# Paths as a nine-row product on TensorE, a reordered opening, later outputs and a third side buffer in a convolution stage

## Chip, cores and metric

One core of one Trainium2 chip runs the whole program. Its engines are TensorE (PE, with its weight loads as PEld), VectorE (DVE), ScalarE (ACT), GpSimd (POOL) and SyncE (SP, which issues all DMAs); each works through its own instructions in program order and waits on semaphores for the others. The metric is the device time of one execution in microseconds (us).

## What is computed

64 sequences of 128 tokens and 256 features pass through a cross attention, a mixture of experts, an alignment with a context and a convolutional feed-forward block, each added to the residual `x`. The change lies in the last two:

```python
def _align_one(small, large):
    D = _pairwise_euclidean(small, large)
    R = _dtw_cost(D)                       # dynamic time warping
    i_idx, j_idx, valid = _backtrack(R, T_small, T_large)
    contrib = small[i_idx] * valid[:, None].astype(small.dtype)
    return jnp.zeros((T_large, d), dtype=small.dtype).at[j_idx].add(contrib)
...
def _L1_ffn_ref(x, w1, conv_w, conv_b, w2):
    h = bit_linear(x, w1)                  # rows quantised to 8 bits, ternary weights
    h = depthwise_conv1d(h.transpose(0, 2, 1), conv_w, conv_b)   # 3 taps
    h = jax.nn.silu(h.transpose(0, 2, 1))
    return bit_linear(h, w2)
...
x = x + _L1_xattn_ref(ctx_1024, _layernorm(x, axis=-1))
x = x + _L1_ffn_ref(_layernorm(x, axis=-1), L1_ffn_w1, L1_ffn_conv_w, L1_ffn_conv_b, L1_ffn_w2)
```

The path of a sequence crosses column t between two bounds. So the alignment's result is a product of the context with a 128 x 128 matrix of zeros and ones (`path_sb`): an entry is 1 where the column number lies between that token's lower and upper bound. Tokens' bounds are neighbouring entries of one table, `entries` (64 sequences x 129).

## The kernel before

Four stages follow one another: attention, experts, `align` (the warping table row by row on DVE, then the way back), and `conv_ffn`. The change touches the last two.

**The end of `align`.** The table is compared in eight chunks of 16 rows. For a chunk, DVE writes `falls` and then `left` (`compare`), PE sums both with `places` into two banks (`gather`, L1536 and L1542), DVE scans the 1024 columns of both banks (`trace`, L1657), PE takes differences (`differ`), ACT copies them (`rises`), and after the last chunk DVE walks back through 128 rows (L1692). Chunks 0 to 6 lie beside the table's rows; the last one stands alone.

**The convolution.** The 64 sequences are 16 groups of four (`GB = 4`, `NG = 16`), and the 1024 hidden features are 8 tiles, so a step n is tile m = n % 8 of group g = n // 8. All engines run the same loop `for n in STEPS`, and at step n each does its own part of a software pipeline: PE makes hidden tile n (`hidden`, L1869) and turns tile n-4 (`turn_hidden`, L1879); ACT makes the middle and side taps of tile n-1 (`taps`, L2003 and L2007) and the SiLU of n-3 (L2014); DVE adds the left tap of n-2 (`tap`, L2145), takes the maxima of tile n-5 (L2150) and scales tile n-14 (L2171); POOL adds the side of n-2 (`add_side`, L2251) and rounds tile n-15 (L2259). The remaining work of a group is hung on certain values of m:

- the path of group g+3, all on ACT: `path_distance` (m = 0, L1952, four ops of 128 columns), `path_gap` (m = 2, L1960, four more), `path_entry` (m = 4, L1969, one op of 512);
- `expand(g, half)` on PE multiplies path and context (L1843), at m = 7 and m = 1; DVE adds it to `x_all` (`add_expanded`) and takes the moments, POOL the inverse deviation, ACT normalises (`normalise`, L1978, m = 5), DVE finds the scale (`find_scale`, m = 6), ACT scales up (`scale_up`, m = 7), POOL scales back (`whole_units`), PE transposes (`turn`, m = 2 and 5), ACT and DVE split it into a leading and a trailing part (L1995, L2137);
- the outputs: `output` on PE (L1904, 16 matmuls, m = 7 of group g+2 and m = 1 of g+3), `weigh_out` on ACT, `finish` on POOL (L2274), `store` on SP. `hidden_scale` on DVE (m = 4) writes the hidden scale and its inverse `inv2`, in two buffers.

Ahead of the loop stands an opening, in which groups 0, 1 and part of 2 are prepared. PE's order there is `expand(0,0)`, `expand(0,1)`, `expand(1,0)`, `turn(0,0)`, `turn(0,1)`, `expand(1,1)`, `expand(2,0)`, and only then the first `hidden`. ACT makes the paths of groups 0 and 1, the leading parts of group 0, then `normalise(1)`, `scale_up(1)` and the path of group 2. A `side` buffer (two of them) is free again when POOL has added it; the bank `ex_ps` is shared by all `expand` calls but one.

## Time and profile before

| what | value |
|---|---|
| median of 3 runs | 3388.7 us (3388.69 to 3393.39) |
| the profiled execution's own time | 3391.26 us |
| its span, first to last instruction | 3389.5 us |
| busy share of the span | PE 91%, DVE 72%, ACT 53%, POOL 38% |
| mean granted TensorE clock | 0.956 of full speed |
| last instruction of `align` to the end | 2957 us to 3389.5 us |

The shares are averages over four stages. In attention and experts PE is busy throughout; in the convolution it isn't. All positions in time below are microseconds from the span's start.

### The profile page before, as it was taken

What the parts mean: (1) busy time and instruction counts of PE and PEld (TensorE: products, weight loads), DVE (VectorE), ACT (ScalarE), POOL (GpSimd) and SP (SyncE); (2) the same over time, 40 slices, a digit from 0 to 9 for tenths busy, and PEclk for the clock granted to TensorE, in tenths of its full rate; (3) what the DMA queues carried; (4) which work ended last, traced back from release to release, by engine and by line L of the source; (5) the groups of instructions that cost most, each with busy time, mean ns of one, the idle gap of its engine ahead of it and who ended that gap; (6) DMA issues with size and microseconds to landing.
All of it is one profiled execution on the core that took longest, in us unless ns stands there. A gap on an engine that the chain in (4) does not pass through costs nothing. (4 is left out here: it accounts for less than half of the span.)

```text
span 3389.5 us, 63898 instructions
## 1 busy us (share of the span) xinstructions
PE 3082.9 (91%) x23092; PEld 2669.3 (79%) x23092; DVE 2443.4 (72%) x5410; ACT 1787.2 (53%) x4638; POOL 1296.7 (38%) x1194
## 2 busy tenths in 40 slices
PE   6999999999999999999998999999999953158887
PEld 5888888888888888888887888888888841046665
DVE  5666666666666666666666787878787759769998
ACT  5565655555555555555554333333333326179996
POOL 2333333333333333333332333333333320058886
PEclk9999999999999999999999999999999975589999
DMA  5000000000000000000001112121212151011101
GB/s 159 5 8 5 8 5 8 5 7 5 8 5 8 5 8 5 8 5 8 4 5 57 58 51 64 51 66 50 65 54 61 58 80 42 1 31 38 50 32 38
DMA packets 108535, 103.81 MB, mean 31 GB/s; under 512 B 26560, under 2 KB 87488, under 8 KB 108224
## 3 DMA queue, kind: packets, MB, share of 16 engines
q1 hardware_dynamic: 108224, 99.72, 10.2%
q8 instruction: 188, 3.08, 0.4%
q14 instruction: 123, 1.01, 0.1%
HBM read 86.55 MB, written 13.14 MB: 29 GB/s over the span
## 5 line engine op out<-in xcount | busy, mean ns | idle before, releaser
L794 POOL TENSOR_TENSOR attention_prob<-attention_prob,attention_inv_sums 128x1024 f32<-128x1024 f32 x256 | 479.6, 1894 | 399.8 <-DVE attention_inv_sums L652 399.8
L504 ACT ACTIVATE attention_prob<-attention_turns,attention_neg_max 128x256 f32<-128x256 f32 x1024 | 467.6, 482 | 175.3 <-DVE attention_neg_max L643 175.3
L1371 POOL TENSOR_TENSOR experts_hidden_lo<-experts_weighed,experts_hidden_hi 128x512 fp32r<-128x512 f32 x192 | 255.0, 1328 | 531.4 <-ACT experts_hidden_hi L1124 531.4
L659 DVE COPY attention_probT<-attention_turns 128x512 f32<-128x512 f32 x512 | 329.0, 684 | 163.1 <-PE attention_turns L380 163.0
L346 PE MATMUL attention_turns<-kv_hi,wkv 128*128 128x512 f32 x1024 | 374.1, 406 | 0.0
L643 DVE TENSOR_REDUCE attention_neg_max<-attention_turns 128x2 f32<-128x512 f32 x512 | 318.1, 684 | 45.2 <-PE attention_turns L370 44.3
L1124 ACT ACTIVATE experts_hidden_hi<-experts_weighed 128x512 fp32r<-128x512 f32 x192 | 121.4, 632 | 404.1 <-DVE experts_weighed L1261 404.1
L314 PE MATMUL attention_turns<-wkv,kv_hi 128*128 128x512 f32 x1024 | 329.8, 403 | 2.1 <-DVE kv_lo L677 2.1
L495 ACT COPY attention_v<-attention_turns 128x512 f32<-128x512 f32 x256 | 149.9, 585 | 311.1 <-PE attention_turns L314 311.1
L380 PEld LDWEIGHTS attention_turns<-ident,attention_prob 128*128 128x128 f32 x2048 | 240.0, 141 | 36.6 <-POOL attention_prob L794 3.2
L380 PE MATMUL attention_turns<-ident,attention_prob 128*128 128x128 f32 x2048 | 265.9, 273 | 2.8 <-POOL attention_prob L794 2.8
L396 PE MATMUL attention_heads_out<-attention_probT,attention_v 128*64 128x128 f32 x4096 | 253.6, 277 | 0.8 <-DVE attention_probT L659 0.8
L396 PEld LDWEIGHTS attention_heads_out<-attention_probT,attention_v 128*64 128x64 f32 x4096 | 222.6, 137 | 18.2 <-DVE attention_probT L659 1.2
L346 PEld LDWEIGHTS attention_turns<-kv_hi,wkv 128*128 128x128 f32 x1024 | 192.6, 188 | 55.3 <-issue 21.6
L652 DVE RECIPROCAL attention_inv_sums<-attention_row_sums 128x4 f32<-128x4 f32 x256 | 44.5, 174 | 265.2 <-ACT attention_prob L504 265.2
L781 POOL TENSOR_TENSOR kv_lo<-attention_kv_full,kv_hi 128x256 fp32r<-128x256 f32 x124 | 90.4, 729 | 373.1 <-ACT kv_hi L473 373.1
L469 ACT ACTIVATE attention_kv_full<-attention_turns,attention_ln_cols 128x128 f32<-128x128 f32 x256 | 102.1, 449 | 223.7 <-PE attention_turns L307 223.7
L504 ACT ACTIVATION_READ_ACCUMULATOR attention_prob<-attention_turns,attention_neg_max 128x1 f32 x1024 | 219.9, 215 | 0.0
L625 DVE SCALAR_TENSOR_TENSOR attention_k_lo<-attention_turns,attention_k_hi 128x512 fp32r<-128x512 f32 x256 | 177.1, 692 | 57.6 <-ACT attention_k_hi L487 50.3
L1025 PE MATMUL experts_out<-experts_down_hi,experts_hidden_hi 128*128 128x256 f32 x768 | 215.2, 280 | 1.0 <-POOL experts_hidden_lo L1371 1.0
L1025 PE MATMUL experts_out<-experts_down_lo,experts_hidden_hi 128*128 128x256 f32 x768 | 215.2, 280 | 0.0
L1025 PE MATMUL experts_out<-experts_down_hi,experts_hidden_lo 128*128 128x256 f32 x768 | 214.9, 280 | 0.0
(287 smaller groups left out, 8948.1 us busy)
## 6 DMA issues: line engine op xcount, KB each, us to landing
experts_spread<-shares SPq DMA_DIRECT2D x256, 128.0 KB, 3.0
attention_ctx<-in_ctx SPq DMA_DIRECT2D x32, 256.0 KB, 2.7
experts_far_ctxT<-in_ctxT SPq DMA_DIRECT2D x32, 256.0 KB, 3.6
weights_ctx<-in_ctx SPq DMA_DIRECT2D x16, 512.0 KB, 3.9
out<-conv_x_out SPq DMA_DIRECT2D x15, 512.0 KB, 2.9
x_all<-in_x SPq DMA_DIRECT2D x7, 1024.0 KB, 9.2
first_x<-norms SPq DMA_DIRECT2D x16, 256.0 KB, 3.1
dist<-experts_far SPq DMA_DIRECT2D x16, 256.0 KB, 2.5
```

What stands on the lines that cost most here:

```text
L314: made = pe.matmul(out, left[l](k), right[r](k), start=n == 0, stop=n == 3 * KD - 1)
L346: made = pe.matmul(bank[:, :].rearrange("p (e c t) -> p c e t", e=2, c=2), wkv_p[l][:, k, w:w + P], (kv_hi, kv_lo)[r][p % 2][:, k, :, :, : ...
L380: made = pe.transpose(bank[:, (2 * h + t) * P:(2 * h + t + 1) * P], prob[n % 2][:, 2 * g + h, t * P:(t + 1) * P], ident[:, :])
L396: made = pe.matmul(heads_out[o * HEAD:(o + 1) * HEAD, (QT * e + m) * TOK:(QT * e + m + 1) * TOK], v[:, home, e, t, h, :], probT[e][:, h, t ...
L495: act.copy(v[:, 0:2 + pj % 2:1 + pj % 2, e, t, :, :].rearrange("p q h c -> p q (h c)"), bank_of("v", c)[:, :].rearrange("p (q c) -> p q c" ...
L504: made = act.activation(prob[n % 2][:, h, :], bank_of("s", 2 * n + e)[:, m * 256:(m + 1) * 256], ACT.Exp, bias=neg_max[:, n % 2, 2 * e + m ...
L625: return dve.scalar_tensor_tensor(lo, view, scale, hi.bitcast(F32), ALU.mult, ALU.subtract)
L643: made = dve.tensor_reduce(neg_max[:, n % 2, 2 * e:2 * e + 2], bank_of("s", 2 * n + e)[:, :].rearrange("p (h c) -> p h c", h=2), AX.X, ALU ...
L659: dve.tensor_copy(probT[n % 2][:, 2 * g:2 * g + 2].rearrange("p h t c -> p (h t c)"), bank_of("t", 2 * n + g)[:, :]).then_inc(p_copied, 1)
L794: pool.tensor_tensor(prob[n % 2][:, :, :], prob[n % 2][:, :, :], inv[:, n % 2, :].unsqueeze(2).broadcast_to([P, QH, 2 * TOK]), ALU.mult).t ...
L1025: made = pe.matmul(out_ps[i // 2][:, (i % 2) * DIM:(i % 2 + 1) * DIM], l[n % 3][:, i * TOK:(i + 1) * TOK], down_w[r][:, m, :], start=t == ...
L1371: pool.tensor_tensor(hid_lo[n % 3][:, :], weighed[n % 2], hid_hi[n % 3][:, :].bitcast(F32), ALU.subtract).then_inc(hid_split, 1)
```

## The change

In `conv_ffn`:

1. **Paths.** For groups 3 to 15 the three ACT steps are replaced. With lower and upper bound a and b of a token, the number (t - a)(b - t) at column t isn't negative inside the path. It is t(a + b) - ab - t*t, a sum of nine products for four sequences: POOL forms a + b and ab for all sequences (`bound_terms`), SP writes them to DRAM and reads them back as rows (`term_rows`), POOL builds the other operand once (`term_shape`), and one fp32 matmul a group with nine rows and 512 columns makes the numbers in `ex_ps` (`form`, m = 3). ACT takes relu(-number) from the bank (`path_outside`, m = 4) and relu(1 - 4 * that) (`path_entry`, m = 5). The paths of groups 0 to 2 are made on DVE by two comparisons a sequence (`first_path`).
2. **Opening.** PE does `expand(1,1)` ahead of `turn(0,k)`, and `expand(2,0)` behind the first `hidden`. `normalise(1)`, `scale_up(1)`, `find_scale(1)` and the scaling back of group 1 move into steps 1 to 3 of the loop, the last of them from POOL to DVE; `turn(1,k)` moves to m = 4 and 6. A small SiLU on ACT stands at the front.
3. **Outputs.** `output` moves from m = 7 (of group g+2) and 1 to m = 0 and 2 (both of g+3), `weigh_out` from m = 0 and 2 to 1 and 3, `finish` from 1 and 3 to 2 and 5, `store` from 4 to 6; `inv2` has three buffers.
4. **Side.** Three `side` buffers in place of two.

In `align`: `gather` takes the matmuls on `falls` first and waits for `left` only behind them, and the last chunk's scan is two scans of one bank each, of which the first releases `differ` and `rises` of its bank.

The core of the diff:

```diff
@@ align: gather and trace
-                pe.wait_ge(compared, c + 1)
                 if c:
                     pe.wait_ge(scanned, c)
...
-                    for weight, flags in ((minus_far, left), (minus_half, falls)):
+                for weight, flags, ready in ((minus_half, falls, fallen), (minus_far, left, compared)):
+                    pe.wait_ge(ready, c + 1)
+                    for b in reversed(range(2)):
...
+                for r in (slice(0, 2 * HC),) if c < CHUNKS - 1 else (slice(HC, 2 * HC), slice(0, HC)):
@@ conv_ffn: SP
+            sp.wait_ge(terms_made, 1)
+            sp.dma_start(terms.rearrange("k b t -> b k t"), sums[:, :, :]).then_inc(terms_stored, 16)
+            sp.wait_ge(terms_stored, 16)
+            sp.wait_ge(ones_set, 1)
+            for k in range(2):
+                sp.dma_start(term_rows[GB * k:GB * k + GB, :, :], terms[k, GB * FORMED:].rearrange("(g b) t -> b g t", b=GB)
+                             ).then_inc(terms_loaded, 16)
             load_ctx(2)
@@ conv_ffn: PE
+            def form(g):
+                if g == FORMED:
+                    pe.wait_ge(terms_loaded, 32)
+                    pe.wait_ge(shape_made, 1)
+                pe.wait_ge(x_added, 2 * g)
+                pe.matmul(ex_ps[:, :], term_rows[:, g - FORMED, :], shape[:, :, :].rearrange("p b t -> p (b t)"),
+                          start=True, stop=True).then_inc(form_made, 1)
...
             expand(1, 0)
+            expand(1, 1)
             for k in range(KD):
                 turn(0, k)
-            expand(1, 1)
-            expand(2, 0)
             for n in STEPS:
...
+                if not n:
+                    expand(2, 0)
...
+                if m == 3 and live(g + 3):
+                    form(g + 3)
...
-                if m == 7 and live(g - 2):
-                    output(g - 2, 0)
-                if m == 1 and 0 <= g - 3 < LAST:
+                if m == 0 and 0 <= g - 3 < LAST:
+                    output(g - 3, 0)
+                if m == 2 and 0 <= g - 3 < LAST:
                     output(g - 3, 1)
@@ conv_ffn: ACT
+            def path_outside(g):
+                act.wait_ge(form_made, g - FORMED + 1)
+                if g > FORMED:
+                    act.wait_ge(path_made, g + 1)
+                act.activation(outside[:, :, :].rearrange("p b t -> p (b t)"), ex_ps[:, :], ACT.Relu, scale=-1.0
+                               ).then_inc(outside_made, 1)
...
-                if n >= 2:
-                    act.wait_ge(side_added, n - 1)
-                act.activation(side[n % 2][:, :, :], h, ACT.Copy, scale=cw[:, m, 2:3]).then_inc(side_made, 1)
+                if n >= SIDES:
+                    act.wait_ge(side_added, n - SIDES + 1)
+                act.activation(side[n % SIDES][:, :, :], h, ACT.Copy, scale=cw[:, m, 2:3]).then_inc(side_made, 1)
...
+            act.activation(acc[0][:, 0, :], column[:, :], ACT.Silu)
             for k in range(KD):
                 leading_part(0, k)
-            normalise(1)
-            scale_up(1)
-            path_distance(2)
-            path_gap(2)
-            path_entry(2)
@@ conv_ffn: DVE
+            def first_path(g, seqs):
...
+                    made = dve.tensor_scalar(path_sb[g % 2][:, i, :], column[:, :], bounds[:, 1, b:b + 1], None,
+                                             ALU.is_ge)
...
+                    made = dve.scalar_tensor_tensor(path_sb[g % 2][:, i, :], column[:, :], bounds[:, 0, b:b + 1],
+                                                    path_sb[g % 2][:, i, :], ALU.is_le, ALU.mult)
@@ conv_ffn: POOL
+            def bound_terms():
+                pool.tensor_tensor(sums[:, 0, :], entries[:, 0:TOK], entries[:, 1:], ALU.add)
+                pool.tensor_tensor(sums[:, 1, :], entries[:, 0:TOK], entries[:, 1:], ALU.mult).then_inc(terms_made, 1)
+                pool.memset(term_rows[:, :, :], 1.0).then_inc(ones_set, 1)
...
+            bound_terms()
             inverse_std(0)
             inverse_std(1)
+            term_shape()
```

PE's queue at the opening of the convolution, before. `conv_expand`, `conv_turned` and `conv_out_ps` are PSUM banks, the digits number buffers; the first row turns the path bounds, the last two are the first hidden tile.

```order
L1824 MATMUL conv_expand<-ident,path_entries 128x64 x2
L1843 MATMUL conv_expand<-weights_ctx0,conv_path0 128x256 x2
L1843 MATMUL conv_turned<-weights_ctx0,conv_path0 128x256 x2
L1843 MATMUL conv_expand<-weights_ctx1,conv_path1 128x256 x2
L1854 MATMUL conv_turned<-ident,conv_xn0 128x128 x4
L1854 MATMUL conv_out_ps<-ident,conv_xn0 128x128 x4
L1843 MATMUL conv_expand<-weights_ctx1,conv_path1 128x256 x2
L1843 MATMUL conv_expand<-weights_ctx0,conv_path0 128x256 x2
L1869 MATMUL conv_h_ps0<-conv_xT_hi0,weights_w1_ternary 128x512
L1869 MATMUL conv_h_ps0<-conv_xT_lo0,weights_w1_ternary 128x512
```

The same place of the changed kernel.

```order
L1843 MATMUL conv_expand<-ident,path_entries 128x64 x2
L1862 MATMUL conv_expand<-weights_ctx0,conv_path0 128x256 x2
L1862 MATMUL conv_turned<-weights_ctx0,conv_path0 128x256 x2
L1862 MATMUL conv_expand<-weights_ctx1,conv_path1 128x256 x4
L1882 MATMUL conv_turned<-ident,conv_xn0 128x128 x4
L1882 MATMUL conv_out_ps<-ident,conv_xn0 128x128 x4
L1897 MATMUL conv_h_ps0<-conv_xT_hi0,weights_w1_ternary 128x512
L1897 MATMUL conv_h_ps0<-conv_xT_lo0,weights_w1_ternary 128x512
```

The expansions of group 1 now stand together ahead of the transposes, and nothing of group 2 stands ahead of the first hidden tile.

PE's queue where one group follows another in the steady part, before. `conv_out_ps` is the output's bank, `conv_xT_hi1` belongs to the next group's first hidden tile.

```order
L1879 MATMUL conv_hidden_turned<-ident,conv_act_h0 128x128 x4
L1843 MATMUL conv_expand<-weights_ctx1,conv_path1 128x256 x2
L1904 MATMUL conv_out_ps<-weights_w2_ternary,conv_hq0 128x256 x16
L1869 MATMUL conv_h_ps2<-conv_xT_hi1,weights_w1_ternary 128x512
L1869 MATMUL conv_h_ps2<-conv_xT_lo1,weights_w1_ternary 128x512
```

The same place of the changed kernel.

```order
L1862 MATMUL conv_expand<-weights_ctx1,conv_path1 128x256 x2
L1897 MATMUL conv_h_ps2<-conv_xT_hi1,weights_w1_ternary 128x512
L1897 MATMUL conv_h_ps2<-conv_xT_lo1,weights_w1_ternary 128x512
L1897 MATMUL conv_h_ps2<-conv_xT_hi1,weights_w1_ternary 128x512
L1897 MATMUL conv_h_ps2<-conv_xT_lo1,weights_w1_ternary 128x512
L1907 MATMUL conv_hidden_turned<-ident,conv_act_h0 128x128 x4
L1932 MATMUL conv_out_ps<-weights_w2_ternary,conv_hq0 128x256 x16
```

The 16 output matmuls stood between the last tile of a group and the first of the next; they now stand behind the next group's first tile and its turned tile.

ACT's queue in a steady group, from step m = 2, before. `conv_acc` and `conv_side` are the taps, `conv_act_h` the SiLU, `conv_gap` and `conv_path` the path.

```order
L1960 ACTIVATE conv_gap0<-conv_gap0,conv_neg_reach 128x128 x4
L2024 ACTIVATE conv_x_out0<-conv_out_ps,conv_h_inv0 128x256 x2
L2003 ACTIVATE conv_acc2<-conv_h_ps0,weights_conv_b,weights_conv_w 128x512
L2007 ACTIVATE conv_side0<-conv_h_ps0,weights_conv_w 128x512
L2014 ACTIVATE conv_act_h1<-conv_acc0 128x512
L1995 ACTIVATE conv_xT_hi0<-conv_turned 128x512
L2033 CAST conv_hq1<-conv_h_whole1 128x512
L2003 ACTIVATE conv_acc3<-conv_h_ps1,weights_conv_b,weights_conv_w 128x512
L2007 ACTIVATE conv_side1<-conv_h_ps1,weights_conv_w 128x512
L2014 ACTIVATE conv_act_h1<-conv_acc1 128x512
L1969 ACTIVATE conv_path0<-conv_gap0,weights_ones 128x512
```

And of the changed kernel, from step m = 3.

```order
L2016 ACTIVATE conv_xT_hi1<-conv_turned 128x512
L2054 CAST conv_hq0<-conv_h_whole0 128x512
L2045 ACTIVATE conv_x_out1<-conv_out_ps,conv_h_inv2 128x256 x2
L2024 ACTIVATE conv_acc3<-conv_h_ps1,weights_conv_b,weights_conv_w 128x512
L2028 ACTIVATE conv_side1<-conv_h_ps1,weights_conv_w 128x512
L2035 ACTIVATE conv_act_h0<-conv_acc1 128x512
L1983 ACTIVATE conv_outside<-conv_expand 128x512
L2024 ACTIVATE conv_acc0<-conv_h_ps2,weights_conv_b,weights_conv_w 128x512
L2028 ACTIVATE conv_side2<-conv_h_ps2,weights_conv_w 128x512
L2035 ACTIVATE conv_act_h0<-conv_acc2 128x512
L1999 ACTIVATE conv_xn0<-x_all,conv_shift,conv_rstd 128x256 x4
L1990 ACTIVATE conv_path1<-conv_outside,weights_ones 128x512
```

The eight small path operations are gone, one of 512 columns from the bank has come, and the path's last operation stands behind the normalisation of m = 5.

## Rows read from the trace of the kernel before

**Rows 1.** Windows, one for each stretch, busy time of each engine in it.

```profile
core 0: us, PE busy (x) PEld busy (x) DVE busy (x) ACT busy (x) POOL busy (x), PEclk, DMA share, GB/s
2957.50:2993.00 35.50, 10.56 (x30) 7.31 (x31) 15.71 (x46) 16.42 (x43) 7.31 (x13) 0.60 0.09 30
2993.00:3013.70 20.70, 14.54 (x66) 10.81 (x65) 13.36 (x27) 18.34 (x34) 8.41 (x11) 0.91 0.08 25
...
3108.40:3133.50 25.10, 20.49 (x119) 15.44 (x117) 23.44 (x48) 24.62 (x52) 21.81 (x28) 0.93 0.13 43
3133.50:3156.40 22.90, 18.61 (x118) 14.47 (x116) 20.99 (x42) 22.73 (x46) 18.56 (x24) 1.00 0.14 47
...
3300.40:3324.30 23.90, 19.32 (x115) 14.53 (x113) 21.75 (x44) 20.95 (x40) 20.61 (x26) 0.93 0.07 23
...
3345.20:3389.50 44.30, 30.94 (x203) 23.81 (x200) 32.40 (x60) 23.93 (x45) 25.36 (x29) 0.91 0.15 49
```

**Rows 2.** Waits by engine and line, six groups, 3108.4 to 3252.6.

```profile
PE conv_hidden_turned L1879 <- DVE conv_h_absmax_part L2150: 15.2, 21, 2.7
...
DVE conv_h_absmax_part L2150 <- PE conv_hidden_turned L1879: 4.4, 6, 1.3
...
DVE conv_acc L2145 <- ACT conv_side L2007: 2.4, 6, 0.6
ACT conv_side L2007 <- POOL conv_acc L2251: 2.0, 5, 0.6
```

**Rows 3.** Timeline of the convolution's opening.

```profile
2958.07 0.27 ACT L1943 COPY conv_path_bounds<-conv_expand 128x128 f32<-128x128 f32 x1 [62.00 <-PE conv_expand L1824]
...
2961.34 2.04 PE L1843 MATMUL conv_expand<-weights_ctx,conv_path 128*128 128x256 f32 x4 [3.31 <-ACT conv_path L1969]
...
2977.58 0.69 DVE L2137 TENSOR_TENSOR conv_xT_lo<-conv_out_ps,conv_xT_hi 128x512 fp32r<-128x512 f32 x1 [0.16 <-ACT conv_xT_hi L1995]
...
2982.60 2.07 ACT L1978 ACTIVATE conv_xn<-x_all,conv_shift,conv_rstd 128x256 f32<-128x256 f32 x4 [5.05 <-POOL conv_shift L2245]
...
2986.51 1.70 ACT L1987 ACTIVATE conv_x_whole<-conv_xn,conv_x_scale 128x256 int8<-128x256 f32 x4 [1.83 <-DVE conv_x_scale L2125]
...
2990.72 0.72 ACT L1969 ACTIVATE conv_path<-conv_gap,weights_ones 128x512 f32<-128x512 f32 x1
...
2991.54 2.05 PE L1843 MATMUL conv_expand<-weights_ctx,conv_path 128*128 128x256 f32 x4 [12.92 <-ACT conv_path L1969]
...
2993.02 0.99 PE L1869 MATMUL conv_h_ps<-conv_xT_hi,weights_w_ternary 128*128 128x512 f32 x1
```

**Rows 4.** Groups of ACT's instructions in the same six groups.

```profile
L1960 ACT ACTIVATE conv_gap<-conv_gap,conv_neg_reach 128x128 f32<-128x128 f32 x24 | 7.8, 425 | 0.0
L1952 ACT ACTIVATE conv_gap<-conv_column,conv_off_middle 128x128 f32<-128x128 f32 x24 | 7.7, 412 | 0.0
L1995 ACT ACTIVATE conv_xT_hi<-conv_turned 128x512 fp32r<-128x512 f32 x12 | 7.2, 604 | 0.0
L1969 ACT ACTIVATE conv_path<-conv_gap,weights_ones 128x512 f32<-128x512 f32 x6 | 4.6, 765 | 0.0
```

**Rows 5.** Timeline inside one steady group.

```profile
3132.72 1.28 ACT L1952 ACTIVATE conv_gap<-conv_column,conv_off_middle 128x128 f32<-128x128 f32 x4
...
3133.88 0.84 ACT L2024 ACTIVATE conv_x_out<-conv_out_ps,conv_h_inv 128x256 f32<-128x256 f32 x2
...
3144.15 1.07 DVE L2163 TENSOR_SCALAR conv_h_inv<-conv_h_absmax,weights_mean 128x4 f32<-128x4 f32 x1
```

**Rows 6.** Timeline of group 14, DVE and POOL.

```profile
3334.30 2.04 DVE L2157 TENSOR_SCALAR conv_h_absmax<-conv_h_absmax 128x4 f32<-128x4 f32 x1
...
3334.66 1.11 POOL L2251 TENSOR_TENSOR conv_acc<-conv_acc,conv_side 128x508 f32<-128x508 f32 x1
...
3335.69 0.63 POOL L2259 CAST conv_hq<-conv_h_whole 128x512 bf16<-128x512 int8 x1
```

**Rows 7.** Timeline of the alignment's last chunk.

```profile
2888.02 0.61 PE L1536 MATMUL align_entry_ps<-align_places,align_ident 128*128 128x512 bf16 x1 [3.96 <-DVE align_left L1648]
...
2891.22 2.29 DVE L1657 TENSOR_TENSOR_SCAN align_entered<-align_goes_on,align_entry_ps 128x1024 bf16<-128x1024 bf16 x1 [3.25 <-PE align_entry_ps L1542]
```

More of the change, by code:

```diff
@@ L1545, in gather @@
                                     weight[:, s * SEQS:(s + 1) * SEQS], flags[:, a:a + 2 * HC - 1:2, :],
-                                    start=False, stop=flags is falls, skip_group_check=True)
+                                    start=False, stop=flags is left, skip_group_check=True)
                 made.then_inc(gathered, 1)
             def differ(c):
-                pe.wait_ge(scanned, c + 1)
                 if c:
@@ L1713, in conv_ffn @@
         bounds = st.sb("path_bounds", [P, 2, SEQS])
-        off_middle = st.sb("off_middle", [P, SEQS])
-        neg_reach = st.sb("neg_reach", [P, SEQS])
-        gap = [st.sb(f"gap{i}", [P, GB, TOK]) for i in range(2)]
+        sums = st.sb("bound_terms", [SEQS, 2, TOK])
+        term_rows = st.sb("term_rows", [2 * GB + 1, NG - FORMED, TOK])
+        shape = st.sb("term_shape", [2 * GB + 1, GB, TOK])
+        outside = st.sb("outside", [P, GB, TOK])
         path_sb = [st.sb(f"path{i}", [P, GB, TOK]) for i in range(2)]
@@ L1730, in conv_ffn @@
         x8 = [st.sb(f"x_whole{i}", [P, GB, DIM], mybir.dt.int8) for i in range(2)]
-        acc = [st.sb(f"acc{i}", [P, GB, TOK]) for i in range(4)]
-        side = [st.sb(f"side{i}", [P, GB, TOK]) for i in range(2)]
+        acc = [st.sb(f"acc{i}", [P, GB, TOK]) for i in range(ACCS)]
+        side = [st.sb(f"side{i}", [P, GB, TOK]) for i in range(SIDES)]
         act_h = [st.sb(f"act_h{i}", [P, TILES, GB * TOK]) for i in range(2)]
@@ L1735, in conv_ffn @@
         amax2 = st.sb("h_absmax", [P, GB])
-        inv2 = [st.sb(f"h_inv{i}", [P, GB]) for i in range(2)]
+        inv2 = [st.sb(f"h_inv{i}", [P, GB]) for i in range(3)]
         q2 = st.sb("h_scale", [P, GB])
@@ L2073, in act_program @@
+                if n == 2:
+                    scale_up(1)
+                if m == 4 and live(g + 3):
+                    path_outside(g + 3)
+                if m == 5 and live(g + 3):
+                    path_entry(g + 3)
                 if tile(n - 15) and rounder(n - 15) == "ACT":
                     round_tile(n - 15)
-                if m == 0 and 0 <= g - 3 < LAST:
+                if m == 1 and 0 <= g - 3 < LAST:
                     weigh_out(g - 3, 0)
-                if m == 2 and 0 <= g - 3 < LAST:
+                if m == 3 and 0 <= g - 3 < LAST:
@@ L2199, in dve_program @@
             first_scale_up()
-            first_whole_units()
+            first_whole_units(0)
+            add_expanded(1, 1)
+            moments(1)
             for k in range(KD):
                 trailing_part(0, k)
-            add_expanded(1, 1)
-            moments(1)
-            find_scale(1)
+            first_path(2, range(GB))
             for n in STEPS:
@@ L2307, in build @@
     norms = nc.dram_tensor("norms", (1, GB * TOK), F32, kind="Internal").ap()
+    terms = nc.dram_tensor("bound_terms", (2, SEQS, TOK), F32, kind="Internal").ap()
     dve_step, pool_step = Steps(nc, "dve_step"), Steps(nc, "pool_step")
@@ L2320, in build @@
             align(nc, dve_step, pool_step, dist, entries, weights, ident)
-            conv_ffn(nc, dve_step, pool_step, x_all, ident, half, ctx, entries, weights, out)
+            conv_ffn(nc, dve_step, pool_step, x_all, ident, half, ctx, entries, weights, terms, out)
 def kernel(**inputs):
```

155 lines of the change are left out of this document (79 added, 76 removed).

## The prediction

> **What bounds the kernel now.** The change lies in the convolution, from 2957.5 to 3389.5, so I read windows cut at the first hidden matmul of a group [rows 1]. In two steady groups (3108.4 to 3156.4, 48.0 us) ACT is busy 24.62 + 22.73 = 47.35 us, DVE 44.43, POOL 40.37, PE 39.10. A group takes 24.0 us on average, 25.1 and 22.9 in turn. ACT has 0.33 us a group left: it is the bound, with DVE close behind at 22.2. The waits of six groups [rows 2] fit: ACT waited 2.0 us, all for a side buffer that POOL hadn't freed; DVE waited 4.4 us for turned tiles and 2.4 us for ACT's side taps. PE waits for DVE (15.2 us), so PE has room.
>
> The opening is another matter [rows 1]: 35.5 us from 2957.5 to the first hidden tile at 2993.0, with every engine under half busy. The timeline [rows 3] shows why. Group 0's input is ready when DVE writes its second trailing part, 2977.58 + 0.69 = 2978.3. But PE's queue has `expand(2,0)` ahead of the first `hidden`, and that waits for the path of group 2, which ACT makes only behind the normalisation (2982.60) and scaling up (2986.51) of group 1: path at 2990.72, expansion at 2991.54, first hidden at 2993.02. So 14.7 us are lost to order alone.
>
> **The change part by part.**
>
> *Alignment's end.* The first gather matmul starts at 2888.02, right behind `left`, and the scan at 2891.22, so 18 matmuls cost 3.2 us [rows 7]. Now 10 of them (`places`, `falls`) don't wait for `left`. The eight on `left` are some 8/18 of 3.2 = 1.4 us; those on `falls` start 1.1 us before `left` ends and last as long, which leaves 0.3 to wait. So the scan starts 1.4 to 2.3 us earlier on paper, less what doesn't fit: I take 0.9. The scan's 2.29 us are halved on the path, 1.1 less. Term: -2.0 (bounds -1.1, for the scan alone, and -3). Chunks 0 to 6 lie beside the table's rows: nothing, and if the extra order harmed them DVE would show a wait for `gathered`.
>
> *First path.* Before, ACT and DVE need 3.0 us from the bounds (2958.34) to the first expansion (2961.34) [rows 3]. Now DVE does four operations of 128 columns for a pair. They aren't in the trace; a DVE operation of 512 columns takes 0.69 [rows 3], so 0.2 to 0.3 each, about 1.1 us, 1.9 less than before. But POOL then does two operations of 128 columns and a memset of 1664. From POOL's 1.11 us for 508 columns with two inputs and 0.63 for 512 with one [rows 6], that is 0.6 + 2.0 us, until about 2960.6. And DVE can be held by POOL: at 3334.30 a DVE tensor_scalar on 4 columns took 2.04 us, until the last of POOL's back-to-back instructions ended (3335.69 + 0.63) [rows 6]; an op of the same kind took 1.07 at 3144.15 [rows 5]. The comparisons with `is_ge` are tensor_scalar too. So I take no gain, with bounds 0 and -1.9.
>
> The Trainium skill, page "SBUF — State Buffer", section "Who interferes with whom", says that such an operation in a two-port mode and a GpSimd instruction exclude each other, whoever is first, for the whole instruction. It adds that a VectorE instruction with two SBUF inputs is blocked only by a GpSimd instruction that reads SBUF. The trace agrees with the first (2.04 and 1.07 us); none of its rows shows the second, by which the `is_le` operations of group 2's path would also wait for POOL's `term_shape`.
>
> *Opening.* The two expansions of group 1 stand together ahead of the transposes; DVE adds the second one (about 1.8 us) ahead of the trailing parts, where it otherwise waits for PE and ACT. So group 0's input stays at 2978.3, and the first hidden tile starts there: -14.7 (bounds -12.6, if one hold of 2.04 lands on this chain, and -16.6, with the 1.9).
>
> *Group 0.* What stood ahead of the loop now lies in it: normalisation 2.07, then DVE's scale (2984.67 to 2986.51, 1.84), then scaling up 1.70 [rows 3], then scaling back on DVE, about 1.2, before group 1 can be turned. That is a serial chain of 6.8 us, with tiles 1 to 4 queued behind its parts on ACT and DVE. ACT had 18.34 busy of 20.7 us there [rows 1]; it gets 3.8 and loses 1.85 (below), so 20.3. The chain starts behind tile 0's taps and runs beside PE and POOL; I take +2.7 (bounds 0 and +6.8). `term_shape` on POOL, two one-input and four two-input operations of 512 columns, 1.2 + 4.4 = 5.6 us [rows 6], fits before the first `add_side` is due. The three new DMAs and their round trip have over 20 us before `form(3)`; `load_ctx(2)`, queued behind them on SP, waits for group 0's expansions (until about 2965) anyway.
>
> *Groups 1 to 12.* On ACT a group loses L1952, L1960 and L1969: (7.7 + 7.8 + 4.6)/6 = 3.35 us [rows 4], less the 0.12 by which each overlaps its successor (2.72 + 1.28 against 3.88 [rows 5]), 3.0 us. It gets `path_entry` back, 0.65, and one operation of 512 columns from a bank, like L1995: 0.60 - 0.12 = 0.48. Net -1.85, so ACT needs 23.7 - 1.85 = 21.8 us, and DVE at 22.2 becomes the bound. If DVE loses as much as ACT does now, 0.33, a group takes 22.55: -1.45, twelve times: -17.4. Bounds: -0.6 (only long groups gain, next part) and -1.8 (DVE without a wait). PE gets `form`, about two expansions (2.05 for four [rows 3]) = 1.0, to 20.6 of 22.5: covered by its wait for DVE. The outputs, 16 matmuls at m = 7 and 1, stood between tiles for which DVE waits; behind the first tile they fall where DVE is busy with `add_expanded`, which should take most of DVE's 4.4 us of waits, and the third buffer ACT's 2.0 and DVE's 2.4 [rows 2]. These make it possible to reach DVE's floor; they aren't added again. `finish` at m = 5 still meets `hidden_scale` on DVE at m = 4, so I leave the hold of 1.07 us, which is in the 44.43, as it is.
>
> *Group 13 and the end.* Group 13 has no path on ACT already, and takes 23.9 [rows 1]; from outputs and side buffers -1.2. The last 44.3 us: outputs one step later, but the last group's stay: 0 (bounds +-1).
>
> Sum: -2.0 - 14.7 + 2.7 - 17.4 - 1.2 = -32.6. Against the profiled execution's 3391.3 (span 3389.5) that is 3358.7; the median before is 2.6 less, so 3356.1: **3356 us**.
>
> **The rivals.**
>
> A: *only half of ACT's relief arrives.* Group 13 is the test that the trace has: 3.0 us less on ACT than a long group, and only 25.1 - 23.9 = 1.2 us shorter; the short groups (22.9) are within 0.7 us of DVE's floor. If that holds, six long groups give 1.2 each: -7.2 in place of -17.4, total -22.4, **3366**. Against it: outputs and side buffers changed too, and group 13 had 1.0 us and more of their waits. Chance 0.24.
>
> B: *the opening trips over POOL.* The path of group 2 on DVE waits for `term_shape`, PE stands at `expand(2,0)` between tiles 0 and 1: +5.6, **3362**. For it: the 2.04 us [rows 6]; against: POOL waits for itself between its operations, which lets DVE in. By the page's rule on two SBUF inputs this would be the likelier. Chance 0.07.
>
> C: *more.* DVE at 22.2 or less and the chain in group 0 hidden: -2 - 16.6 - 21.6 - 1.5 = -42, **3347**. Chance 0.07.
>
> D: *slower.* POOL's later `finish` puts its back-to-back runs onto the four small tensor_scalar operations of m = 4 and 6 on DVE. At two holds of 2.04 a group in place of one of 1.07 in every second, DVE needs 22.2 + 3.5 = 25.7: 1.7 above today, thirteen times +22, less 14 = +8, **3397**. It decides from 25.1 a group. Speaks for it: group 14's 2.04; against: one such case in 16 groups. Chance 0.03.
>
> E: *no change that can be told.* A and B together with the 6.8 of group 0 given in full and holds of 1 us a group: about -3. Chance 0.04.
>
> **How the numbers follow.** The forecast has 0.55; its own range, from the bounds of the large terms taken half, is 3349 to 3364. With A, B and most of C the range of 8 in 10 is 3346 to 3371. A measurement tells 0.2%, 6.8 us, from no change. All but D and E are faster by more: 0.93; same 0.04; slower 0.03.
>
> **What would show it.** In the profile after: the first hidden matmul some 17 us earlier (with the alignment's 2), near 2976; the way back of the alignment starting 2 us earlier; groups of 22.3 to 22.9 us without the turns of 25.1 and 22.9; ACT busy near 21.8 of them with idle time behind it, DVE at 97% or more; no wait of ACT for POOL at the side taps; `conv_outside` about 0.6 us. The prediction is wrong if DVE's small tensor_scalar operations take over 1 us in each group (D), if the groups stay at 23.4 with DVE waiting (A), if PE waits for a path behind tile 0 (B), or if group 0 lasts over 26 us.

## The result, and the profile after

The changed kernel takes 3373.3 us (median of four runs, 3373.2 to 3373.8) against 3391.05 (median of four, 3388.7 to 3393.9): a ratio of 0.9948, 95% interval 0.9930 to 0.9965, so 17.8 us faster. The forecast was 32.6 us; 3373.3 lies 2 us above the range of 3346 to 3371. The profiled execution takes 3373.19 us with a span of 3371.5.

Windows of the kernel after, in the columns of [rows 1]: the opening up to the first hidden matmul, group 0, two held groups and one that isn't (cut at DVE's first `add_expanded`, L2112), and the end.

```profile
core 0: us, PE busy (x) PEld busy (x) DVE busy (x) ACT busy (x) POOL busy (x), PEclk, DMA share, GB/s
2957.50:2973.10 15.60, 6.78 (x22) 4.28 (x20) 14.18 (x43) 1.20 (x2) 3.17 (x7) 0.61 0.21 67
2973.10:2999.30 26.20, 19.84 (x70) 13.83 (x70) 18.75 (x42) 21.66 (x41) 15.49 (x18) 0.80 0.06 20
3067.39:3091.63 24.24, 21.05 (x119) 16.39 (x118) 22.92 (x46) 22.31 (x42) 20.23 (x26) 0.92 0.15 44
3091.63:3115.88 24.25, 21.04 (x118) 16.37 (x118) 22.93 (x45) 22.34 (x42) 20.24 (x26) 0.92 0.13 45
3164.38:3187.39 23.01, 19.85 (x115) 15.23 (x114) 21.96 (x45) 21.53 (x41) 20.24 (x26) 0.95 0.14 47
3325.80:3371.50 45.70, 31.30 (x216) 24.35 (x216) 33.31 (x61) 24.89 (x46) 26.25 (x31) 0.96 0.13 47
```

ACT has its relief (22.3 busy of 24.24, about 2 us idle), yet the group is about as long as before (24.0 us on average). The whole convolution in three stretches says where the time is and isn't. They are cut at ACT's copy of the bounds (L1943, after L1975) and at DVE's first `add_expanded` in groups 3 and 13. Windows of before, then of after:

```profile
2958.07:3058.91 100.84, 59.67 (x267) 44.00 (x268) 70.05 (x156) 79.96 (x167) 48.58 (x63) 0.80 0.09 27
3058.91:3300.21 241.30, 199.94 (x1169) 153.35 (x1168) 223.55 (x441) 237.70 (x482) 202.46 (x251) 0.95 0.13 42
3300.21:3389.50 89.29, 67.39 (x424) 51.67 (x422) 72.52 (x133) 63.27 (x116) 63.37 (x75) 0.94 0.11 36
```

```profile
2952.97:3043.16 90.19, 62.68 (x270) 44.59 (x271) 78.85 (x180) 65.38 (x119) 53.86 (x68) 0.84 0.10 31
3043.16:3282.28 239.12, 207.79 (x1181) 161.57 (x1180) 226.52 (x442) 223.23 (x412) 202.47 (x251) 0.94 0.13 43
3282.28:3371.50 89.22, 67.53 (x434) 52.60 (x432) 71.70 (x133) 63.96 (x117) 63.30 (x75) 0.95 0.10 36
```

Up to the copy 5.1 us are gained, in the opening with groups 0 to 2 10.65, in groups 3 to 12 only 2.2, behind them 0.1: 18.0, the difference of the spans.

The timeline of DVE in one group after shows the inside of the 24.24 us: two waits for turned tiles, 0.71 and 0.23, and `h_inv` (L2183), four columns wide, at 1.06 us.

```profile
3072.20 0.69 DVE L2170 TENSOR_REDUCE conv_h_absmax_part<-conv_hidden_turned 128x4 f32<-128x512 f32 x1 [0.71 <-PE conv_hidden_turned L1907]
...
3077.99 0.69 DVE L2170 TENSOR_REDUCE conv_h_absmax_part<-conv_hidden_turned 128x4 f32<-128x512 f32 x1 [0.23 <-PE conv_hidden_turned L1907]
...
3079.14 0.18 DVE L2180 RECIPROCAL conv_h_scale<-conv_h_absmax 128x4 f32<-128x4 f32 x1
3079.24 1.06 DVE L2183 TENSOR_SCALAR conv_h_inv<-conv_h_absmax,weights_mean 128x4 f32<-128x4 f32 x1
3080.33 0.69 DVE L2191 TENSOR_TENSOR conv_h_whole<-conv_act_h,conv_broadcast 128x512 int8<-128x512 f32 x1
...
3086.48 0.47 DVE L2141 TENSOR_SCALAR conv_x_inv<-conv_x_absmax 128x4 f32<-128x4 f32 x1
```

POOL's timeline beside it:

```profile
3079.18 1.09 POOL L2299 TENSOR_TENSOR conv_acc<-conv_acc,conv_side 128x508 f32<-128x508 f32 x1
```

L2183 ends at 3080.30, L2299 at 3080.27: the small operation is held for POOL's whole instruction. Without holds the two take 0.20 and 0.17 us. So the group is 24.24 = 22.14 of DVE's own sequence + 0.86 + 0.30 held + 0.94 waiting for PE. In groups 3 to 12 L2183 is held seven times (before, L2163: six times, beside POOL's `finish`) and L2141 every time, beside POOL's cast (before, L2121: never).

DVE's wait for PE has to do with PE's clock, too. Windows of 2 us of the same group and the next one's start:

```profile
3066.00:3068.00 2.00, 2.00 (x6) 1.49 (x5) 2.00 (x4) 1.73 (x3) 1.57 (x2) 0.50 0.00 0
3070.00:3072.00 2.00, 2.00 (x17) 1.73 (x15) 1.49 (x3) 1.25 (x4) 2.00 (x3) 1.00 0.00 0
3086.00:3088.00 2.00, 0.52 (x3) 0.09 (x1) 1.89 (x6) 2.00 (x5) 0.92 (x2) 1.00 0.74 262
3090.00:3092.00 2.00, 2.00 (x6) 1.58 (x5) 2.00 (x4) 1.97 (x4) 1.34 (x2) 0.50 0.00 0
```

PE is busy without a gap in the first half of a group and has 0.52 of 2 us at the end of it; then the granted clock is 0.50, 1.2 GHz, while the next group's expansion and first hidden tile pass. In the kernel before, the first hidden tile of each of these ten groups ran at full clock (1.65 us, the sum of its four matmuls): the fall of the clock came with the change, by the outputs' new place (e3 has them back and every first tile at full clock).

### The profile page after: what moved, and what is told of

Its sections match the earlier page's. It is cut to its first block and busy times, and to the rows that moved or that the text cites. A ratio compares the mean times of both kernels' runs of the same rounds, so it can differ in the third digit from the quotient of the medians.

```text
span 3371.5 us, 63871 instructions
## 1 busy us (share of the span) xinstructions
PE 3090.4 (92%) x23118; PEld 2677.0 (79%) x23118; DVE 2453.9 (73%) x5435; ACT 1760.1 (52%) x4520; POOL 1303.3 (39%) x1199
```

## Experiments

A run is told here by three numbers: the median, its ratio to the kernel before on the same chip, and the length of groups 3 to 12 in its trace (before 241.3, after 239.1). The last is the sharpest, since it leaves out what differs ahead: in these profiles the copy of the bounds comes anywhere between 2951.3 and 2955.0 with the same alignment code. A small operation is called held when it takes longer than in the groups where POOL leaves it alone.

**e1: another form for the small operations.**

```
-dve.tensor_scalar(inv2[g % 3][:, :], amax2[:, :], w_mean[:, 1:2], None, ALU.mult)
+dve.scalar_tensor_tensor(inv2[g % 3][:, :], amax2[:, :], w_mean[:, 1:2], ones4[:, :], ALU.mult, ALU.mult)
 (and so for inv1, x_unit and amax2)
```

> The changed kernel, with the four small tensor_scalar operations of VectorE in find_scale and hidden_scale (128x4) written as scalar_tensor_tensor with a constant second input; the values are the same. Theory (holds): in the changed kernel's groups 3 to 12 the L2183 operation takes 1.07 us in place of 0.20 in seven groups, because it is in flight with POOL's add_side, and L2141 0.47 in place of 0.17 in each, behind POOL's cast. If only the tensor_scalar form is held, groups 3 to 7, 9 and 10 get 1.17 us shorter and 8, 11 and 12 0.3: about -9, 3364, and the operations take 0.2 us. Rival 1 (any small DVE operation is held by a POOL instruction that runs): they still take 1.07 and 0.47, time 3373. Rival 2 (PE is the real bound): they take 0.2 us but DVE's waits for turned tiles grow from 0.94 to about 2 us a group, time 3371 to 3373.

3377.6 us (3370.0 to 3379.4), ratio 0.9964 (0.9951 to 0.9978); 235.9 us. DVE's timeline of e1, and POOL's beside it:

```profile
3124.35 1.07 DVE L2185 SCALAR_TENSOR_TENSOR conv_h_inv<-conv_h_absmax,weights_mean,conv_ones 128x4 f32<-128x4 f32 x1
3125.45 0.69 DVE L2194 TENSOR_TENSOR conv_h_whole<-conv_act_h,conv_broadcast 128x512 int8<-128x512 f32 x1
```

```profile
3124.31 1.09 POOL L2304 TENSOR_TENSOR conv_acc<-conv_acc,conv_side 128x508 f32<-128x508 f32 x1
```

Rival 1's outcome came: the new form is held as long, here in four groups of ten, and L2143 still takes 0.46. Whether L2185 is caught depends on less than a tenth of a microsecond: held, it starts 0.04 to 0.07 us behind `add_side` (here 3124.35 against 3124.31); where it starts 0.06 us or more ahead of it, it takes 0.19. Held groups take 24.21 to 24.26 us, the others 23.0 to 23.4. That may be what spreads the runs (3370.0 to 3379.4); each run has one trace, so it isn't shown. The Trainium skill, page "SBUF — State Buffer", section "Who interferes with whom", says it so: a two-port operation is excluded by any GpSimd instruction, one with two SBUF inputs by a GpSimd instruction that reads SBUF. Both trace rows agree (1.06 and 1.07 us); so do the operations with one SBUF input, `h_scale` (0.18) and `h_whole`, whose second input is in PSUM (0.69), which were never held. For one of POOL's instructions the trace doesn't agree. It has two inputs of four columns in SBUF and makes the inverse deviation; L2179 starts 0.65 us into its 1.04 us and isn't held, nor is L2185 at its end. A group of e1 that isn't held, POOL first:

```profile
3099.90 1.04 POOL L2275 TENSOR_TENSOR conv_rstd<-conv_var_eps,minus_half 128x4 f32<-128x4 f32 x1
```

```profile
3100.55 0.16 DVE L2179 SCALAR_TENSOR_TENSOR conv_h_absmax<-conv_h_absmax,conv_per 128x4 f32<-128x4 f32 x1
...
3100.84 0.19 DVE L2185 SCALAR_TENSOR_TENSOR conv_h_inv<-conv_h_absmax,weights_mean,conv_ones 128x4 f32<-128x4 f32 x1
```

So rival 1's "any small operation" is too wide on DVE's side, and "a POOL instruction that runs" on POOL's. (Spans on POOL are rough in this profile.)

**e2: outputs in the second half of a group.**

```
-if m == 0 and 0 <= g - 3 < LAST:
+if m == (4 if g < NG else 0) and 0 <= g - 3 < LAST:
     output(g - 3, 0)
-if m == 2 and 0 <= g - 3 < LAST:
+if m == (6 if g < NG else 2) and 0 <= g - 3 < LAST:
     output(g - 3, 1)
```

> The changed kernel, with the outputs of group g - 3 at steps 4 and 6 of a group in place of 0 and 2 (weighing at 5 and 7, POOL's finish at 6 and at the next 0), for the groups before the tail. Theory (PE's queue is the bound in the first half of a group and idle in the second): DVE waits 0.94 us a group for turned tiles, because PE is busy without a gap from the eighth tile's turn to the fourth, 13.4 us, and starts that stretch at half clock (first hidden tile 2.87 us in place of 1.75) after 3 us with little to do. With 3.5 us of outputs in the second half the first tile takes 1.75 us, DVE's wait goes to under 0.2, and a group loses 0.8 us or so: 12 groups, -10, 3363; a hold on DVE's small operations may come or go with POOL's finish (+-0.9 a group, so 3353 to 3373). Rival (the place of the outputs does not matter, or they delay the tiles of steps 5 to 7 in turn): 3373 or up to 3380, with waits of DVE for turned tiles in the second half of a group.

3374.1 us (3369.0 to 3374.7), ratio 0.9952 (0.9939 to 0.9964); 232.7 us, 6.4 less. No small operation is held (0.24 at most), the clock over these groups is 0.99. But the theory, waits under 0.2 us a group, was wrong, and the rival right about them: they are 0.5 us in the first of the ten groups and about 1.1 in the others, at other tiles (about 8 and 16 us into the group). What shortened the groups is the 9.1 us of holds that are gone, not a wait. And behind group 12 the kernel takes 95.15 us in place of 89.22: PE stands once for 3.48 and once for 1.73 us for the whole units (L2313), which POOL makes behind `finish`. The waits of e2 in these ten groups:

```profile
PE conv_turned L1882 <- POOL conv_xn L2313: 13.2, 9, 1.7
DVE conv_h_absmax_part L2170 <- PE conv_hidden_turned L1907: 10.3, 19, 0.6
```

**e3: outputs, weighing, `finish` and store back at their old steps; e4: that with two side buffers.**

```
-if m == 0 and 0 <= g - 3 < LAST:
-    output(g - 3, 0)
-if m == 2 and 0 <= g - 3 < LAST:
+if m == 7 and live(g - 2):
+    output(g - 2, 0)
+if m == 1 and 0 <= g - 3 < LAST:
     output(g - 3, 1)
 (weigh_out at 0 and 2, finish at 1 and 3, store at 4; in e4 also SIDES = 2)
```

> The changed kernel, with the outputs, their weighing, POOL's finish and the store back at the steps of the kernel before (7 and 1; 0 and 2; 1 and 3; 4). My prediction's reason (the outputs' later place takes DVE's waits for turned tiles away) gives 1.0 us a group back: 12 groups, 3385. Theory now: the outputs' move exchanged one wait for another: it cost PE its clock at the first tile and put POOL's add_side on L2183 in nearly every group, and saved 0.66 us of waits. Back at the old steps the first hidden tile takes 1.66 us, DVE waits 1.6 us a group for PE, L2183 is held in about half of the groups: 22.15 + 1.6 + 0.43 = 24.2 against 24.24, so 3373 +-4.

> As e3_outputs_back, with two side buffers in place of three: in the steady groups this is the kernel before with nothing changed but the path from one PE product. Theory (ACT is no longer the bound, so that the third buffer hides nothing but ACT's and DVE's 0.4 us a group): e3 plus 0 to 0.4 us a group, 3373 to 3378. Rival (the path alone brings nothing in steady groups, since DVE's own 22.15 us plus PE's waits plus holds are as long as before): groups of 24.6 and 23.5 in turn as before, which with 14.9 + 5.1 us of the opening and the alignment less is 3391 - 17 = 3374. If the third buffer was worth what I gave it (2.0 and 2.4 us in six groups, 0.7 a group), e4 is 8 us above e3.

e3: 3373.8 us (3372.5 to 3375.0), ratio 0.9956 (0.9943 to 0.9968); 237.1 us. e4: 3379.2 us (3378.1 to 3382.1), ratio 0.9973 (0.9962 to 0.9984); 240.9 us. The outputs' later place brought nothing on balance, in the trace rather the reverse (237.1 against 239.1): it took away 4.2 us of DVE's waits for ACT and brought 5.6 us more of holds and 0.7 more of waits for PE. In e3 PE's clock is full at every first tile (1.66 us, where after has 2.28 to 2.88 in eight of these ten groups), and still DVE waits for PE as in the kernel before (8.1 us in the ten groups, before 8.85), since an output stands ahead of the tile that it needs. The third side buffer is worth 3.8 us in the trace and 5.4 in the medians: with two, ACT stands 8.7 us for a free one, and DVE's waits for ACT are 9.2 us in place of 4.2. And e4 is, in these groups, the kernel before with the path from one product. Its windows of the first stretch and of groups 3 to 12:

```profile
2954.13:3044.96 90.83, 63.98 (x280) 45.75 (x281) 78.73 (x180) 65.35 (x118) 53.83 (x68) 0.83 0.10 31
3044.96:3285.90 240.94, 203.68 (x1170) 152.44 (x1169) 220.99 (x441) 221.47 (x411) 202.58 (x251) 0.96 0.13 42
```

ACT is busy 16 us less than before (221.5 against 237.7) and the ten groups are 0.4 us shorter: the form alone brings nothing there. DVE even waits longer for ACT (9.2 us against 5.1), because ACT now waits for POOL to free a side buffer; three groups are held in place of six. A kernel before with nothing but a third side buffer was not run.

**e5: the kernel before, with the alignment's part alone.** The edit is the `align` part of the change and nothing else.

> The kernel before with only the alignment's part of the change. In the two traces the stretch from the start of the last left to the first product of the way back went from 8.51 us (2886.74 to 2895.25) to 5.42 (2884.73 to 2890.15): 3.1 us less, of which 2.1 is the scan's wait and 1.0 the halved scan; another 2.0 of the 5.1 us by which the way back began earlier was there before the last chunk and varies from execution to execution. Theory: 3.1 us less than before, nothing from the rest. Prediction on record: 2.0. Rival: the order of the sums shortens the chunks too, and 5.1 us come.

3387.8 us (3384.0 to 3390.8), ratio 0.9995 (0.9985 to 1.0004): too small to tell by the medians. In the trace of e5 the stretch from the last `left` to the first product is 5.43 us, where the kernel before has 8.51 (2886.74 to 2895.25, DVE's L1648 and L1692) and the one after 5.42:

```profile
2885.69 1.22 DVE L1649 TENSOR_TENSOR align_left<-align_cost,align_best 128x1024 bf16<-128x1024 f32 x1
2888.08 2.33 DVE L1661 TENSOR_TENSOR_SCAN align_entered<-align_goes_on,align_entry_ps 128x512 bf16<-128x512 bf16 x2 [1.17 <-PE align_entry_ps L1543]
2891.12 0.35 DVE L1696 SCALAR_TENSOR_TENSOR align_products<-align_columns,align_path,align_rise 64x127 f32<-64x127 f32 x1 [0.70 <-ACT align_rise L1591]
```

So 3.1 us are the change's. The other 2.0 of the 5.1 are chance of that execution: they are there at the alignment's first `left` already (2789.4 and 2787.4), and from the first to the last it takes 97.3 us in both, so the chunks before the last gained nothing. e5 also separates the opening: its stretch from the copy to group 3 is 100.98 us, e4's 90.83.

**e6: ACT's relief taken back.**

```
+if m in (0, 1, 2) and live(g + 3):
+    if n:
+        act.wait_ge(load_done, 3 * g + m)
+    act.activation(load[:, :, :], column[:, :].unsqueeze(1).broadcast_to([P, GB, TOK]), ACT.Abs
+                   ).then_inc(load_done, 1)
```

> The changed kernel with the relief of ACT taken back: three more ACT operations of 512 columns in steps 0, 1 and 2 of each group up to 12 (some 1.8 us a group), written to a tile that nobody reads. Prediction on record (ACT at 23.7 of 24.0 us was the bound, so its relief of 1.85 is worth 1.45 a group): the time goes up by 1.45 to 1.8 a group, +19 to +23, 3392 to 3396. Theory now (before and after, a group is DVE's own 22.15 us, plus what its small operations are held by POOL, plus its waits for turned tiles; ACT only has to stay under that): 24.24 us hold 21.8 + 1.8 of ACT, so 0 to +4, 3373 to 3377.

3377.9 us (3372.8 to 3378.5), ratio 0.9963 (0.9951 to 0.9976), against 0.9948 and, in e9, 0.9957 for the kernel after. The ten groups take 238.5 us (six held). Groups of ACT's instructions and two windows of e6:

```profile
L2083 ACT ACTIVATE conv_load<-conv_column 128x512 int8<-128x512 f32 x30 | 19.6, 653 | 0.0
```

```profile
3068.55:3091.82 23.27, 20.74 (x120) 16.44 (x120) 22.06 (x45) 22.74 (x44) 20.24 (x26) 0.94 0.13 46
3091.82:3116.08 24.26, 21.06 (x119) 16.48 (x118) 22.94 (x45) 24.26 (x47) 20.25 (x26) 0.92 0.13 45
```

The added operations last 1.96 us a group. In the second window ACT is busy 24.26 of 24.26, and the group is as long as without. Over the ten groups ACT is busy 235.1 of 238.5 us, the same 98.6% as in the kernel before (237.7 of 241.3); that is only 11.8 us more than in the kernel after, since the records of back-to-back operations overlap. A busy share of 100% is not a bound: with less to do ACT just stands and waits. On this run the prediction's largest term falls.

**e7: the held operation moved to ACT; e8: e2 and e7 together, with POOL's `finish` at 6 and at the next 2.**

```
+def out_scale(g):
+    act.wait_ge(q2_made, g + 1)
+    ...
+    act.activation(inv2[g % 3][:, :], amax2[:, :], ACT.Copy, scale=w_mean[:, 1:2]).then_inc(inv2_made, 1)
 ...
-    dve_step(dve, dve.tensor_scalar(inv2[g % 3][:, :], amax2[:, :], w_mean[:, 1:2], None, ALU.mult))
```

> The changed kernel with the inverse of the hidden scale (L2183, 128x4) made on ACT at step 6 in place of DVE at step 4. e1 showed that the operation is held in either form, 1.07 us in seven to eight groups. Theory: 1.07 us go from each group in which it was held, 0.2 from the others: about -8.5, 3365, and the groups no longer differ by 0.9. Rival (PE's queue is the bound in the first half of a group): the waits for turned tiles grow by what is freed, 3371 to 3373. Second rival: the hold moves to the operation behind it, L2191, which then takes 1.5 in place of 0.68: 3373.

> Both mends at once: outputs at steps 4 and 6 as in e2, with POOL's finish at 6 and at step 2 of the next group (in e2 it stood at 0, ahead of whole_units, and PE waited 3.5 us in two groups for POOL's whole units), and L2183's work on ACT as in e7. Theory: groups of e2 (23.33) without the 0.2 and with the waits for turned tiles (1.1) halved: 22.6 in place of the 23.9 of the changed kernel, ten times, 3360 (bounds 3355 and 3368). Rival (a slack taken from PE and from the holds goes into a new wait): 23.3 a group, 3368 or more.

e7: 3366.0 us (3363.8 to 3367.1), ratio 0.9930 (0.9918 to 0.9943); 229.1 us, 10.0 less than after, so the theory was right. (The kernel after has the hold in seven groups, e1 in four.) ACT pays 0.3 us a group (L2042, 299 ns). Groups are now 22.3 to 23.6 us, the rest of the waits of these ten groups being

```profile
DVE conv_h_absmax_part L2179 <- PE conv_hidden_turned L1907: 7.7, 14, 0.7
```

e8: 3366.8 us (3364.5 to 3368.4), ratio 0.9933 (0.9920 to 0.9945); 232.8 us. The rival's 23.3 us a group came; its time, 3368 or more, is just missed, because behind group 12 it is the best kernel, 86.87 us. Against e7 the groups have 3.1 us of waits for ACT's side taps and 0.7 for the expansion that e7 hadn't, and 8.6 us of waits for turned tiles in place of 7.7; `find_scale`'s L2150 is held in seven of the ten groups (1.8 us in all, e7 3.0, e2 none).

**e9: the kernel after once more; e10: with ACT's leading part of group 1 ahead of group 2's normalisation; e11: e7 with that; e12: e11 with the outputs in four pieces.**

```
+if n == 5:
+    leading_part(1, 0)
 if m == 5 and live(g + 2):
     normalise(g + 2)
-if m == turn_step(g, 0) + 1 and live(g + 1):
+if m == turn_step(g, 0) + 1 and live(g + 1) and g:
     leading_part(g + 1, 0)
 (e12)
+elif g >= 3 and m in (2, 3, 5, 6):
+    output(g - 3, m // 5, ((m - 2) % 3,))
```

> The changed kernel itself once more, on the chip of e10 to e12, so that they can be compared with it there. 3373 +-3; its profile shows again how many of groups 3 to 12 have the 1.07 us operation L2183 (seven in the first one) and how long the stretch from the copy of the bounds to group 3 is (90.2 us).

> The changed kernel with one ACT operation moved: in group 0 the leading part of group 1's first half stands ahead of the normalisation of group 2 in step 5, no longer behind it. In the changed kernel's trace the transposes of group 1 are done at 2987.8 and ACT copies them at 2991.77, behind the normalisation (2.06 us) and a tile; DVE waits 3.05 us for it. Theory (group 0's extra 5.6 us over before is this order and the serial chain of group 1's scale, not the amount of work): 2 us of the wait go, 3371. Rival (the other links of the chain, DVE's whole units at 2.00 us and POOL, take its place): no change.

> e7 and e10 together: the scale's inverse on ACT, and the leading part first. Sum of both: -7.3 and -2, 3364. Rival: they hit the same wait, 3366.

> e11 with the outputs of a group in four pieces of 8 matmuls, at steps 2, 3, 5 and 6 (weighing at 4 and 7, finish at 5 and at the next 2). In e7 DVE still waits 0.67 us for turned tiles at step 2 in most groups and 0.72 at the last tile in some, about 0.8 a group; PE is at 2.0 us of 2.0 in the first half of a group and idle for 2.3 us in the second. Theory (PE's queue in the first half is what is left): with half of the 3.5 us of outputs moved to the second half and no piece longer than 0.9 us, the waits go under 0.3 a group, ten groups, -5, 3359. Rival (e8 showed it for whole halves: DVE waits 0.8 us at the tile behind an output in the second half): 3364 or more.

- e9: 3376.8 us (3372.6 to 3377.9), ratio 0.9957 (0.9944 to 0.9969); 239.9 us, eight groups held.
- e10: 3376.3 us (3373.4 to 3380.6), ratio 0.9959 (0.9946 to 0.9971); 239.9 us. Against the first trace of the kernel after, DVE's wait for the first part falls from 3.05 to 1.79 and that for the second rises from 1.21 to 2.91: the first wait's gain comes back in the second, and the rival was right that there is no change.
- e11: 3364.5 us (3362.6 to 3368.0), ratio 0.9924 (0.9910 to 0.9937); 229.3 us. It beats both kernels, by 12.3 us the kernel after on the same chip (3376.8), nearly all of it the move of e7, since e10 alone brings nothing.
- e12: 3369.5 us (3369.3 to 3371.7), ratio 0.9940 (0.9928 to 0.9953); 237.4 us. Groups of 23.9 us in place of 22.8 to 23.1, and the waits for turned tiles have become waits for ACT and for the expansion:

```profile
DVE conv_acc L2180 <- ACT conv_side L2032: 8.5, 19, 0.7
DVE x_all L2127 <- PE conv_expand L1862: 3.8, 9, 0.4
```

## Why the prediction was wrong

By its own terms, against the trace: alignment -2.0 forecast, -3.1 measured (e5), with 2.0 of chance on top; opening, group 0 and groups 1 and 2 -14.7 + 2.7 - 2.9 = -14.9, measured -10.65, all of it up to group 2's first `add_expanded`; groups 3 to 12 -14.5, measured -2.2; group 13 and the end -1.2, measured -0.1. Sum -32.6 and -18.05.

**The step that failed is "Groups 1 to 12".** It made ACT the bound from its busy share, 23.7 of 24.0 us, and let DVE's 22.2 be the next one. e6 shows that ACT was not the bound in the changed kernel (1.96 us of work for nothing) and e4 that it was none before (16 us less work, 0.4 us gained). What a group costs is DVE's serial sequence, plus what POOL holds of it, plus its waits. Groups 3 to 12 in these parts, us in all ten (own is what is left of the total):

| run | total | own | held | waits for PE | waits for ACT |
|---|---|---|---|---|---|
| before | 241.3 | 222.1 | 5.3 | 8.85 | 5.1 |
| e4 (form, two side buffers) | 240.9 | 222.0 | 2.6 | 7.1 | 9.2 |
| e3 (and the third) | 237.1 | 221.3 | 3.5 | 8.1 | 4.2 |
| after (and the outputs later) | 239.1 | 221.2 | 9.1 | 8.8 | 0 |
| e6 (and ACT loaded again) | 238.5 | 221.5 | 8.1 | 8.9 | 0 |
| e7 (after, with `h_inv` on ACT) | 229.1 | 218.4 | 3.0 | 7.7 | 0 |

So the change did take away DVE's waits for ACT, by the buffer and the outputs' place and not by ACT's relief, and three quarters of that went into new holds. The forecast of 22.55 against a mean of 23.91 comes apart in three pieces, 0.35 + 0.48 + 0.55 = 1.38 (1.36 but for rounding):
- DVE's own sequence is 22.12 us, not 22.2 - 0.43 of hold = 21.77. Busy time leaves out the short gaps between dependent small operations: in the group at 3067.39, 24.24 - 22.92 busy - 0.94 waited = 0.38.
- Holds: 7 x 0.87 + 10 x 0.30 = 9.1 us in ten groups, 0.91 each; forecast 0.43. The prediction left the hold "as it is". It became more frequent, and `find_scale` got one of its own. e7 took the larger one away, and 10.0 us went: 6.1 of hold, 2.0 of the operation itself, 0.8 of DVE's gaps, and 1.1 of waits that got shorter (8.8 to 7.7).
- Waits for PE, 0.88 us a group; forecast 0.33. The outputs' place "should take most of DVE's 4.4 us of waits" for turned tiles: over the ten groups these were 8.85 us and stayed 8.8. The side buffer did bring 0.38 us a group (e4 against e3).

The "25.1 and 22.9 in turn" that the prediction started from look different from DVE. Cut at its first `add_expanded`, the six groups of the kernel before with a held L2163 take 24.35 to 24.63 us and the four others 23.46 to 23.71. Most of that difference is the hold of 0.87 us and not ACT's work.

**The opening was mis-sized.** The first hidden matmul came at 2973.07, 14.9 us nearer to the copy of the bounds, as forecast. But nothing waits for PE's first tile as such. DVE's next operation in the program, the first `add_expanded` of group 2, came 24.90 us behind the copy in place of 35.62, 10.7 less, because the path of group 2 (DVE, 2972.93 to 2975.7) and its expansion (2975.78) now stand behind that tile: it comes 4.80 us behind the first hidden matmul in place of 0.67. PE's head start was given back in group 0, 26.2 us against 20.7; groups 1 and 2 were 2.1 and 2.8 shorter by PE's tiles. So the 4.3 us missing are rival B's mechanism in a mild form, with DVE as the one that waits (2.18 us for the expansion) and POOL adding only 0.7 to the path (L2104 1.49 against 1.14 us beside `term_shape`, L2099 1.23 against 0.87). The scaling back of group 1 on DVE, forecast at 1.2 us, took 2.00 (L2151). e4 against e5 confirms the size: -10.15.

**Right:** the direction; the mechanism of the alignment (the scan's wait 3.25 to 1.17, size 3.1 in place of 2.0); no gain worth the name on the first path, whose first tensor_scalar pair took 1.65 us beside POOL's memset (2953.37 + 1.47), 0.5 us won in place of 0; `conv_outside` at 0.60 us; no wait of ACT at the side taps; and of the rivals A came nearest with 3366, though its reason (half of ACT's relief arrives) is not what happened: none of it did. Of the signs that the prediction named for its failure, two were there: group 0 over 26 us, and small tensor_scalar operations over 1 us in most groups (D's mechanism, at 0.87 us each and not at two times 2.04; D's 3.5 us also counts what the two operations take unheld, without which it is about 3.2).

**What the clock costs** can be read from e11, in which groups with a slow and a full first tile stand side by side and nothing is held at L2183's place. Two neighbours, the first with a first tile of 2.88 us, the second of 1.75:

```profile
3043.53:3066.64 23.11, 20.79 (x124) 16.25 (x123) 21.82 (x44) 22.35 (x43) 20.23 (x26) 0.96 0.14 46
3066.64:3089.41 22.77, 19.81 (x121) 15.08 (x120) 21.76 (x45) 22.23 (x43) 20.25 (x26) 1.00 0.14 47
```

Four of its ten groups are of the first kind, 23.11 to 23.13 us with 0.92 to 0.95 of waits for PE, five of the second, 22.76 to 22.77 with 0.66 to 0.68. So the clock is some 0.3 of the 0.94 us, and the larger part is there at full clock too.

**Not settled:** no run changed the clock alone in the kernel after, where it may also shift `add_side` against L2183: the two of its groups with a full first tile are not held. And why e12's tap of step 2 waits for ACT was not followed up.

## What to carry to other kernels

- An engine that is 98% busy is a bound only if work added to it costs time. Before an edit is priced by a relief, find in the chain which engine's sequence has no slack, and count that sequence from start to start, not by busy time. A load put back, as in e6, is the cheapest test.
- Price an earlier start at the engine that everything behind it follows, not at the first tile of another.
- In a sequence that bounds, look at each small operation that stands beside POOL. A four-column operation cost 0.87 us in each group in which it was held; moving it to the engine that had been relieved (e7) was worth more than the rest of the change in these groups.
